# Scaling of the normalised queries and keys on GpSimd, and a new split of the PSUM banks, in the third layer's cross-attention of a four-layer kernel

## What is computed

```python
def _ln(t, w, b):
    m = jnp.mean(t, axis=-1, keepdims=True)
    v = jnp.var(t, axis=-1, keepdims=True)
    return (t - m) * jax.lax.rsqrt(v + EPS) * w + b
...
q = _ln((x @ Wq + bq).reshape(b, s1, H, HD), qn_w, qn_b)      # H = 16 heads of HD = 16
...
k = _ln(kv[..., :HD], kn_w, kn_b)
v = kv[..., HD:]
...
ctx = _attn(qT, k..., v...)              # over 112 keys
ctx_dca = _attn(qT, k_dca..., v_dca...)  # over 16 more keys, a softmax of its own
ctx = ctx + DCA_WEIGHT * ctx_dca
return ctx @ Wo + bo
```

## Time and profile before

| | |
|---|---|
| time, median of 3 runs | 2385.31 us (2382.98 to 2386.84) |
| the profiled execution's own time | 2385.19 us |
| its span, from the first to the last instruction | 2383.3 us |
| mean granted clock of PE | 0.938 |
| busy over the span: PE, DVE, ACT, POOL | 86%, 53%, 46%, 37% |
| steps 0 to 63 of layer 3's attention (first and last maxima on DVE) | 1906.70 to 2152.72 us |
| first product of the experts of layer 3 | 2213.70 us |

### The profile page before, as it was taken

How to read it: one execution, slowest core, us unless ns; L and a number is a source line. 1 busy time by engine, 2 the same in 40 slices (tenths; PEclk the granted TensorE clock), 3 DMA queues, 4 the chain that set the end, 5 groups by cost and what they waited for, 6 DMA issues and landing times.

```text
span 2383.3 us, 37985 instructions
## 1 busy us (share of the span) xinstructions
PE 2051.9 (86%) x11533; PEld 1475.8 (62%) x11533; DVE 1272.8 (53%) x3538; ACT 1099.2 (46%) x3319; POOL 886.0 (37%) x808
## 2 busy tenths in 40 slices
PE   6999999878888869969999999888999588883782
PEld 4666666778777746546666566545666366663672
DVE  2556545466776653455565555352333686884233
ACT  4445454246666643345665555332333255551230
POOL 1221212122123145534444536322555312557574
PEclk9999999999999979979999999999999798996896
DMA  9999700243234225620000001233666432324798
GB/s 323 356 352 346 232 1 1 72 89 84 76 83 106 78 75 94 119 66 1 1 1 10 29 1 39 93 113 97 104 103 103 98 81 74 119 86 102 162 183 197
DMA packets 258899, 259.15 MB, mean 109 GB/s; under 512 B 66525, under 2 KB 245989, under 8 KB 257934
## 3 DMA queue, kind: packets, MB, share of 16 engines
q1 hardware_dynamic: 221454, 208.59, 30.3%
q0 software_dynamic: 37248, 48.14, 11.3%
HBM read 114.48 MB, written 150.14 MB: 111 GB/s over the span
## 4 chain that ended last, share of the span: by engine, by line
PE 31%; issue 7%; DVE 7%; DMA 4%; POOL 3%; ACT 2%; SPq 1%; POOLq 0%; DVEq 0%; ACTq 0%
PE ps L135 25%; DMA moe_sum<-xn,work 1%; POOL f_rows L3092 1%; PE ps L584 1%; PE ps L610 1%; DMA moe_sum<-work 1%; PE ps L1966 1%; POOL moe_sum L3189 1%; PE ps L1981 1%; DMA work<-f_rows 1%; ACT work L665 1%; ACT work L2688 1%; POOL rk L467 1%; PE ps L436 0%; SPq L3062 0%
## 5 line engine op out<-in xcount | busy, mean ns | idle before, releaser
L135 PE MATMUL ps<-weights,work 128*128 128x126 f32 (+6 forms) x3188 | 636.0, 336 | 34.5 <-DVE work L1038 18.7
L135 PEld LDWEIGHTS ps<-weights,work 128*128 128x128 f32 (+2 forms) x3188 | 458.2, 198 | 89.3 <-issue 24.9
L135 PE MATMUL ps<-xn_T,weights 128*128 128x512 f32 (+4 forms) x960 | 357.9, 506 | 13.3 <-DVE qvar L729 8.4
L135 PE MATMUL ps<-work,weights 128*128 128x512 f32 (+3 forms) x1152 | 346.4, 435 | 3.6 <-ACT work L674 3.1
L2044 POOL DMA_INDIRECT f_sum<-work x120 | 185.3, 1544 | 182.2 <-ACT work L2005 140.3
L749 POOL TENSOR_TENSOR work<-work,rinv 128x512 f32<-128x512 f32 x128 | 133.3, 1041 | 301.0 <-DVE rinv L700 278.7
L135 PEld LDWEIGHTS ps<-work,weights 128*128 128x128 f32 (+2 forms) x1152 | 172.4, 184 | 78.8 <-issue 68.6
L135 PEld LDWEIGHTS ps<-xn_T,weights 128*128 128x128 f32 (+2 forms) x960 | 149.0, 189 | 108.8 <-issue 87.6
L1006 ACT ACTIVATE work<-ps,n_negm 128x128 f32<-128x128 f32 x512 | 145.7, 378 | 95.6 <-DVE n_negm L1032 93.5
L3092 POOL DMA_INDIRECT f_rows<-ctx,weights x128 | 125.1, 977 | 150.1 <-DVEq L3181 100.4
L135 PE MATMUL ps<-weights 72*128 72x128 bf16 (+6 forms) x790 | 152.3, 320 | 32.5 <-issue 13.5
(11 more groups left out here) (332 smaller groups left out, 3609.4 us busy)
## 6 DMA issues: line engine op xcount, KB each, us to landing
f_rows<-weights SPq DMA_DIRECT2D x25, 2176.0 KB, 19.5
work<-f_rows SPq DMA_DIRECT2D x120, 136.0 KB, 2.6
weights<-in_L_ffn_gate_up_proj SPq DMA_DIRECT2D x29, 384.0 KB, 4.8
f_rows<-weights SPq DMA_DIRECT2D x4, 2592.0 KB, 25.1
work<-f_rows SPq DMA_DIRECT2D x64, 162.0 KB, 3.4
f_sum<-weights SPq DMA_DIRECT2D x4, 2176.0 KB, 15.6
weights<-in_L_ffn_W SPq DMA_DIRECT2D x96, 88.0 KB
weights<-l_parts SPq DMA_DIRECT2D x84, 96.0 KB
```

The source lines that it names most:

```text
L135: return nc.tensor.matmul(out, lhsT, rhs, start=start, stop=stop, skip_group_check=True)
```

## The change

The multiplication by the roots moves from DVE to POOL, under a new signal `l3_root` that DVE gives once the roots stand. The scores rotate over two banks (B4, B5), and wait for the exponentials of step t-2 where they waited for those of t-3. B3, which this frees, takes the turned outputs. With that the products with the values wait for `l3_on_ready` of the block before last (DVE has read the bank) where they waited for `l3_ot_ready` (ACT has copied the turned output), and the turning waits for the copy of the block before it. The exponential of the routing is written one step earlier on ACT for the first six pairs (`EXP3`).

```diff
+    l3_root = signal("narrow_in_ready", 1, B)
...
+    EXP3 = [t - 1 for t in TOP3[:PAIRS - 2]] + TOP3[PAIRS - 2:]
...
-                if t >= 3:
-                    done(pe, l3_p, 0, t - 3)
-                mm(S_BANKS[t % 3], l3_q[:, b % 2, hf, :], ...
+                if t >= 2:
+                    done(pe, l3_p, 0, t - 2)
+                mm(S_PAIR[t % 2], l3_q[:, b % 2, hf, :], ...
...
                 if u % 2 == 0:
-                    done(pe, l3_ot_ready, blk - 2, 0)
+                    done(pe, l3_on_ready, blk - 2, 0)
...
                 done(pe, l3_on_ready, blk, 0)
-                nc.tensor.transpose(out3(blk)[:, 0:P], l3_on[:, blk % 2, :], ident[:]).then_inc(l3_o_tr.sem, 1)
+                done(pe, l3_ot_ready, blk - 1, 0)
+                nc.tensor.transpose(B3[:, 0:P], l3_on[:, blk % 2, :], ident[:]).then_inc(l3_o_tr.sem, 1)
...
             root_steps(link, l3_r[:, b % 2, :], l3_var[:, b % 2, :], l3_t)
             link.close()
-            g = l3_qk[:, b % 2, :].rearrange("p (g d) -> p g d", d=L3HD)
-            nc.vector.tensor_tensor(g, g, l3_r[:, b % 2, :].unsqueeze(2).broadcast_to([P, 32, L3HD]), ALU.mult).then_inc(l3_n_ready.sem, 1)
+            dve.sem_inc(l3_root.sem, 1)
...
+    def l3_norm_pool(pool, t):
+        b = due(t, NORM_AT, 4, B)
+        if b is not None:
+            done(pool, l3_root, b, 0)
+            g = l3_qk[:, b % 2, :].rearrange("p (g d) -> p g d", d=L3HD)
+            nc.gpsimd.tensor_tensor(out=g, in0=g, in1=l3_r[:, b % 2, :].unsqueeze(2).broadcast_to([P, 32, L3HD]), op=ALU.mult)\
+                .then_inc(l3_n_ready.sem, 1)
+
     def l3_pool(pool):
         for t in range(FIRST_STEP, SLOT3[0]):
+            l3_norm_pool(pool, t)
             later_sums_pool(pool, t)
+        normed = SLOT3[0]
         for g in range(PAIRS):
...
+                while normed <= t:
+                    l3_norm_pool(pool, normed)
+                    normed += 1
...
     def f3_route_act(act, t):
-        g = pair_at(t, TOP3)
+        g = pair_at(t, EXP3)
```

More of the change, by code:

```diff
@@ L2585, in l3_pe @@
                     done(pe, kb_in[b % 2], b // 2, 16 * 2 * NB - 1)
-                if t >= 3:
-                    done(pe, l3_p, 0, t - 3)
-                mm(S_BANKS[t % 3], l3_q[:, b % 2, hf, :], l3_kb[:, b % 2, hf, r * NB:(r + 1) * NB, :].rearrange("p j c -> p (j c)"))\
+                if t >= 2:
+                    done(pe, l3_p, 0, t - 2)
+                mm(S_PAIR[t % 2], l3_q[:, b % 2, hf, :], l3_kb[:, b % 2, hf, r * NB:(r + 1) * NB, :].rearrange("p j c -> p (j c)"))\
                     .then_inc(l3_s_mm.sem, 1)
@@ L2687, in l3_act @@
                 for j in range(NB):
-                    nc.scalar.activation(n_p[:, i, j, 0:MAIN], S_BANKS[t % 3][:, j * P:j * P + MAIN], ACT.Exp,
+                    nc.scalar.activation(n_p[:, i, j, 0:MAIN], S_PAIR[t % 2][:, j * P:j * P + MAIN], ACT.Exp,
                                          bias=n_negm[:, i, j:j + 1])
@@ L2697, in l3_act @@
                     done(act, l3_y_mm, g - 2, 0)
-                nc.scalar.activation(l3_ot[:, g % 2, blk % 2, blk // 2 % 2 * P:(blk // 2 % 2 + 1) * P], out3(blk)[:, 0:P], ACT.Copy)\
+                nc.scalar.activation(l3_ot[:, g % 2, blk % 2, blk // 2 % 2 * P:(blk // 2 % 2 + 1) * P], B3[:, 0:P], ACT.Copy)\
                     .then_inc(l3_ot_ready.sem, 1)
@@ L2773, in l3_dve @@
                 done(dve, l3_s_mm, 0, t)
-                bank = S_BANKS[t % 3].rearrange("p (h k) -> p h k", h=NB)
+                bank = S_PAIR[t % 2].rearrange("p (h k) -> p h k", h=NB)
                 done(dve, l3_p, 0, t - 4)
```

## The result

The changed kernel takes 2364.41 us (median of 4 runs, 2360.08 to 2367.29) against 2385.18 for the kernel before: a ratio of 0.991, 95% interval 0.9891 to 0.9929. A second set gave 2363.96 and 0.9906 (0.9889 to 0.9924). The gain is 21 to 22 us where 14.8 were forecast; the measured time lies at the very end of the range (2364): just inside it by the first median, just outside by the second. The profiled execution took 2364.83, its span is 2363.1.

A forecast was written before the change was run, and what follows sets the result against it. DVE was taken as the chain up to step 61, with PE not far behind. Gains of 2.7 + 11.7 + 3.4 less 3.0 given back made 14.8 us, so 2370.5 us, range 2364 to 2379.

The forecast's parts named there:

- The end follows step 61: Experts start a fixed 64.5 us after DVE's slots of step 61, so DVE's gains up to there move the end.
- The exponential: Routing on ACT, steps 20 to 60: DVE's six waits for the routing's exponential go, 11.7 us won.
- The multiplication: Moving it from DVE to POOL wins 0.34 us in each of ten steps, 19 to 55: 3.4 us.
- The banks: PE no longer waits for the copy of the turned output (11.1 us); DVE gains nothing by itself.
- The early steps: Ahead of step 16: the copy of the keys of sequence 3 starts 2.7 us earlier; other gains vanish in PE's wait.
- Given back: Steady steps: keys and PE come late by 0.1 to 0.7 us per eight steps; 5 x 0.6 = 3.0 us lost.
- (c): Rival: no port price on DVE and no PE limit, 20.5 us won, 2364.7 us; chance 0.08.
- (b): Rival: PE and the keys bind much more, half of DVE's gain becomes waits for PE, 2375.5 to 2377.5; chance 0.20.
- (d): Rival: the end doesn't follow as POOL becomes late for pair 5, or PE swallows nearly all, 2381 to 2385; chance 0.06.
- (e): Rival: slower, the multiplication queues behind POOL's indirect DMAs and keys come late, 2387 to 2404 us; chance 0.04.

The follow-up runs named there:

- e9: Kernel before with only the routing's exponential moved ahead of the attention's exponentials and key copies on ACT; won 9.5 us.
- e11: Kernel before with only the bank edits: two score banks, own banks for the turned outputs; won 1.2 us, interval holding zero.
- e13: Changed kernel with the turned outputs back in the bank of the products with the values; ratio 0.9934 to the kernel before.
- e16: Changed kernel with SyncE's sixteen expert-weight issues spread, one pair to each of eight sequences; 2354.6 us, ratio 0.9867 to the kernel before.
- e18: Changed kernel with the expert-weight burst behind the keys of sequence 4; ratio 0.9974 to the kernel before, which took 2420 us in that set.
- e15: Changed kernel with a second wide GpSimd operation, result unused, right behind each multiplication; ratio 0.9934 to the kernel before.

## Why the prediction was wrong, step by step

**The end follows step 61:** right, 237.9 and 237.8 us. Over all profiles of the undisturbed sets this stretch lies between 235.0 and 240.9, so a difference of 3 us in the whole time can come from there.

**The exponential, 11.7 us:** right in mechanism and size. No wait for it is left, and it is 2.1 us in each window at full clock. But this takes for granted that the clock stays, and alone it does not: in e9 it fell in two windows (to 0.50 for 3.4 us, 0.94 over the window), and steps 17 to 61 gained 9.

**The multiplication, 3.4 us:** right. L2866 takes 1.05 (1.1 to 1.25 forecast). All ten steps with a multiplication went from 3.70 to 3.75 us to 3.37 to 3.39, 0.33 a piece against 0.34. The way there is a little different: L2773 takes 0.45 and not 0.6, but DVE, which now gives the signal there, goes from the start of its last operation on the roots to the start of the next in 0.33 and not in 0.22. The hold cost 0.16 of 0.61, and only on the operation with two SBUF operands.

**The banks, nothing: also wrong, by less.** As a whole time e11 shows nothing (1.2 with an interval that holds zero). But PE, rid of its second wait, has the routing's logits ready earlier, and DVE's wait for them shrinks from 2.6 to 1.1 us: "DVE gains nothing by itself" left this out. And the banks take away the second of two waits after which PE's granted clock fell to 0.50 in 7 of 24 windows: with the clock, 3.9 us in e13's profile. I had counted PE's waits as free because DVE was the chain.

**The early steps, 2.7 us:** the wait ahead of step 16 follows the keys' copy as said, and step 16 is 3.4 earlier (from step 0 to 16 3.5 us were won, 2.7 in the second profiles). e16 and e18 show that SP's burst is the cause. From step 16 to 17 another 1.5 came (5.90 to 4.39), but the second profiles have 5.12 before and 4.96 after, so most of this is chance.

**Given back, 3.0 us: this step failed.** I expected 11.7 + 3.4 - 3.0 = 12.1 in steps 17 to 61; 15.2 and 15.1 were measured. DVE's waits for scores, which this step prices, grew by 0.5 us in one pair of profiles and 1.7 in the other, not by 3.0, and the shorter waits for the logits outweigh or nearly outweigh that, so on balance nothing was given back. I took the issue group of 5.96 us in the earlier trace rows as SP's price and put it into all five cycles. In the changed kernel the groups that count take 5.05 in three windows of four:

```profile
2031.49 5.05 SPq L2897 DMA_DIRECT2D weights<-weights  x8
...
2058.84 6.08 SPq L2897 DMA_DIRECT2D weights<-weights  x8
```

From step 40 to 45, behind the long group, DVE took 15.92 us (15.64 forecast), and it waited 0.85 for the scores of step 45; from step 32 to 37, behind a short one, 15.11. Only the window with the 6.08 is 0.8 longer than its neighbours (the first window's 27.87 holds a wait of 0.5 of DVE for itself, which is there before as well). So the chain of the keys was priced rightly for the long group, and the long group is not the rule: of the four such groups before, two were short. And a shortfall of "0.1 to 0.7" had been turned into 0.6 with a guess that two engines' waits add.

The missing 6 us are thus 3.1 in steps 17 to 61 (this step and the logits' wait), 0.7 in the early steps, 1.5 from step 16 to 17 that is mostly chance, and what the medians differ from the profiled executions (20.2 in span, 21 to 22 in medians). Whether the last is more than chance is open.

Of the rivals, (c) named 2364.7, almost the measured time. That is luck: it had no hold on VectorE at all, where L2773 took 0.45 in place of 0.29, and 6.1 for the multiplication, which gave 3.3 in steps 17 to 61. The "port" in its name is shown by no run; they show this hold and its length. (b), (d) and (e) did not occur: PE was ahead, POOL stood idle for 2.93 us ahead of the last train, and POOL was idle, waiting for the roots, ahead of each of its 16 multiplications.

## What to carry to other kernels

Before a chain gets a transfer's price, list all groups of that transfer in the trace, not the one beside the place: here the difference between 5.04 and about 6 us for one group decided whether a step gave back nothing or 0.8 us, and with keys 1.27 us later between 0.5 to 1.5 and 2.7 to 3.9. A wait on an engine off the chain was nearly free here only as long as the clock behind it stayed (e13: 0.4 us in a window at 1.00, 1.5 to 1.9 where it fell to 0.50): look at the granted clock in stretches of 2 us behind each such wait, and compare windows with the same waits. And take away a wait that swallows gains (here a burst of sixteen bulk issues ahead of small urgent ones) before polishing what lies ahead of it: it was worth 9 us.

## What was unexpected in the hardware

The same two waits of TensorE, 1.0 and 0.8 us, were followed by a granted clock of 0.50 for 3.4 us in two of e13's four windows and by 1.00 in the others. SyncE's same eight issues took 5.03 to 6.4 us, and not at random: in the fourteen profiles of the undisturbed sets that show the group of step 41 as one row, it took 5.6 to 6.4. In two of five sets the other engines waited on for TensorE's results after its recorded ends (by 3.4 and 4.2 us in the place shown), with 12 to 21 such waits in steps 17 to 61, and the same kernel took 2419 in place of 2385 us. A VectorE operation with two SBUF operands was held only to the end of the GpSimd operation it met, not through the next one that followed without a gap (e15: it took 0.45 us, as in the changed kernel, and ended 0.15 us after the first of the two).
